# Three reorderings in one kernel: the rounding of an expert chunk on ScalarE, a product on TensorE, an exponential ahead of a rounding

## What is computed

```python
# B=8 batches, S=512 rows, D=512 columns; ctx: 77 rows per batch
x = x + cross_attention(layernorm(x), ctx)       # softmax over one score of the row with its own key (q.k_tok) and 77 with ctx
x = x + ffn(layernorm(x))
def ffn(x):
    q, k, v = (x @ W_qkv + b_qkv) in 16 heads of 32 columns
    attn_out = softmax(q k^T / sqrt(32)) v       # per batch and head, 512 x 512 scores
    gate = softmax(x @ W_gate + b_gate); keep the two largest of 8
    moe_out = sum over the two experts e of gate_e * (x @ W_experts[e] + b_experts[e])
    return attn_out + moe_out
```

## Time and profile before

| | us |
|---|---|
| median of three runs | 1453.66 (1448.44 to 1458.95) |
| the profiled execution | 1453.07 |
| its span, first to last instruction | 1451.4 |
| TensorE busy in the span | 1325.3 |
| VectorE busy | 947.3 |
| ScalarE busy | 910.6 |
| mean granted TensorE clock | 0.962 |

### The profile page before, as it was taken

How to read it: one execution, slowest core, us unless ns; L and a number is a source line. 1 busy time by engine, 2 the same in 40 slices (tenths; PEclk the granted TensorE clock), 3 DMA queues, 4 the chain that set the end, 5 groups by cost and what they waited for, 6 DMA issues and landing times.

```text
span 1451.4 us, 25227 instructions
## 1 busy us (share of the span) xinstructions
PE 1325.3 (91%) x6720; PEld 969.9 (67%) x6721; DVE 947.3 (65%) x2047; ACT 910.6 (63%) x1856; POOL 361.2 (25%) x572
## 2 busy tenths in 40 slices
PE   4989999999799899999999999999998879999987
PEld 4967888888666566656666566665665347777775
DVE  4256788878768878777777777777777623433332
ACT  4123444444338789989899898998999833333332
POOL 0001222222200011210212102120001017777765
PEclk9999999999899999999999999999998779999998
DMA  5005677666664237444464444644449668877873
GB/s 159 1 23 203 244 250 246 244 231 250 211 192 132 51 97 160 95 118 103 105 159 92 119 101 107 159 90 121 101 107 268 233 204 147 144 130 127 144 134 53
DMA packets 111369, 212.44 MB, mean 146 GB/s; under 512 B 28266, under 2 KB 36586, under 8 KB 109140
## 3 DMA queue, kind: packets, MB, share of 16 engines
q1 hardware_dynamic: 82048, 166.13, 38.4%
q0 software_dynamic: 26624, 42.04, 17.3%
q10 hardware_dynamic: 2643, 3.65, 0.8%
HBM read 79.48 MB, written 77.73 MB: 108 GB/s over the span
## 4 chain that ended last, share of the span: by engine, by line
PE 56%; DVE 14%; issue 9%; ACT 8%; DMA 8%; POOL 3%; POOLq 1%; ACTq 0%; DVEq 0%; SPq 0%
PE banks L221 10%; PE banks L223 10%; PE banks L222 10%; PE banks L1073 8%; PE banks L1057 7%; PE banks L1037 7%; DMA out_dram<-plain,score_bias 4%; ACT plain L772 3%; DVE st L1222 3%; ACT banks L762 2%; DMA plain<-h_rows,score_bias 2%; DVE plain L1528 1%; DVE plain L1270 1%; DVE plain L1259 1%; PE banks L1130 1%
## 5 line engine op out<-in xcount | busy, mean ns | idle before, releaser
L221 PE MATMUL banks<-parts 128*128 128x512 f32 (+6 forms) x1108 | 435.4, 393 | 23.6 <-issue 6.6
L223 PE MATMUL banks<-parts 128*128 128x512 f32 (+6 forms) x1108 | 422.1, 381 | 0.0
L222 PE MATMUL banks<-parts 128*128 128x512 f32 (+6 forms) x1108 | 421.8, 381 | 0.0
L1528 DVE TENSOR_REDUCE plain<-banks 128x1 f32<-128x512 f32 x512 | 329.1, 685 | 75.6 <-PE banks L1037 66.0
L762 ACT ACTIVATE banks<-banks,plain 128x512 f32<-128x512 f32 x512 | 339.2, 664 | 25.2 <-DVE plain L1528 23.1
L772 ACT ACTIVATE plain<-banks 128x1024 f32<-128x1024 f32 x256 | 263.0, 1027 | 45.7 <-PE banks L1057 43.9
L221 PEld LDWEIGHTS banks<-parts 128*128 128x128 f32 (+1 forms) x1108 | 213.5, 193 | 66.8 <-issue 33.2
L223 PEld LDWEIGHTS banks<-parts 128*128 128x128 f32 (+1 forms) x1108 | 212.6, 192 | 39.5
L222 PEld LDWEIGHTS banks<-parts 128*128 128x128 f32 (+1 forms) x1108 | 213.7, 193 | 34.1
L1037 PE MATMUL banks<-parts 96*128 96x512 f32 x512 | 207.5, 443 | 23.0 <-ACT banks L762 22.3
L1057 PE MATMUL banks<-parts 104*128 104x512 f32 x512 | 174.6, 423 | 10.3 <-ACT plain L772 10.1
(11 more groups left out here) (180 smaller groups left out, 1495.0 us busy)
## 6 DMA issues: line engine op xcount, KB each, us to landing
parts<-parts SPq DMA_DIRECT2D x384, 128.0 KB, 2.5
experts_split<-parts SPq DMA_DIRECT2D x32, 512.0 KB, 4.2
h_turned<-parts SPq DMA_DIRECT2D x32, 512.0 KB, 2.9
parts<-h_turned SPq DMA_DIRECT2D x32, 512.0 KB, 7.1
parts<-experts_split SPq DMA_DIRECT2D x8, 2048.0 KB, 8.6
plain<-in_x_dram SPq DMA_DIRECT2D x32, 256.0 KB, 4.1
plain<-in_L_ffn_W_experts_dram SPq DMA_DIRECT2D x32, 256.0 KB, 4.2
out_dram<-plain SPq DMA_DIRECT2D x32, 256.0 KB, 2.3
```

What stands on the lines that cost most here:

```text
L221: pe.matmul(out, stat[0], mov[0], start=first, stop=False)
L222: pe.matmul(out, stat[0], mov[1], start=False, stop=False)
L223: return pe.matmul(out, stat[1], mov[0], start=False, stop=last)
L1528: dve.tensor_reduce(nmx[:, k, t:t + 1], bank[SB[t]][:], AX.X, ALU.max, negate=True).then_inc(q["f_max"], 1)
```

## The change

Three places change their order, and nothing is added or removed.

1. In the tile stage ScalarE does `chunk_hi` of tile t directly behind `p_hi` and ahead of `weigh` of the same step; before it was the last work of the step, behind `h2_norm`.
2. In `score` TensorE does the first 512-column chunk of the quadratic form ahead of the eight key products; it was behind them.
3. In the "dense" heads ScalarE does the third exponential E2 ahead of the rounding D; it was behind it.

```diff
             "dense": {"pe": "S0 S1 T2@2 n@1 S2 Da S3 OT T0@1 Db",
-                      "act": "E3@1 t2@2 E0 E1 t0@1 D E2",
+                      "act": "E3@1 t2@2 E0 E1 t0@1 E2 D",
...
             def steps(b, part):
                 for t in range(T):
-                    for d, work in ((-1, p_hi), (0, weigh), (1, h_hi), (2, h_norm), (-2, h2_hi), (-3, gate_out), (-1, h2_norm), (0, chunk_hi)):
+                    for d, work in ((-1, p_hi), (0, chunk_hi), (0, weigh), (1, h_hi), (2, h_norm), (-2, h2_hi), (-3, gate_out), (-1, h2_norm)):
...
+            def own_key(u, c):
+                return prod3(pe, bank[1][:, c * P:D], at(hT[u % 2], sl, c), at(A, sl, c, slice(c * P, D)), c == 0, c == C - 1)
+
             def score(i, u, bb):
 
                 await_ge(pe, "s_step", 4 * i)
                 pe.wait_ge(q["hT_ready"], i + 1)
+                own_key(u, 0)
                 for c in range(C):
...
                 last.then_inc(q["s_keys"], 1)
-                for c in range(C):
-                    last = prod3(pe, bank[1][:, c * P:D], at(hT[u % 2], sl, c), at(A, sl, c, slice(c * P, D)), c == 0, c == C - 1)
+                for c in range(1, C):
+                    last = own_key(u, c)
                 last.then_inc(q["s_full"], 1)
```

## The result

The changed kernel takes 1506.26 us (1504.87 to 1508.78, four executions) against 1452.66 (1448.44 to 1458.95, four) for the kernel before on the same chip: a ratio of 1.037, 95% interval 1.033 to 1.041. The forecast was 1506. The profiled execution took 1504.87 us, its span 1503.2, its mean granted clock 0.944.

What follows compares the result with a forecast made beforehand. It took TensorE to set the tile stage's pace, some 8.6 us a tile, with TensorE and ScalarE nearly level in the heads. Profiled 1453.07 + 56 - 3 = 1506 us; 8-in-10 range 1486 to 1536.

Steps and rivals of the forecast that it cites:

- Part 1, the wait on the load: Tile stage, ScalarE: the moved rounding waits for the chunk's load and delays `weigh`; together +56 us, bounds +41 to +73.
- The loop: Tile stage, per tile: norm to load issue, landing, rounding, `weigh` to next norm; 10.65 us against 8.6, 26 times, +49.6 us.
- The first tiles and the end: Tile stage: tiles 2 to 4, with slower landings, +8 us; from tile 30's exponential to the last value product, -1.6 us.
- both ends of the heads: Head stage rival: bounds of -26 and +16 us come true, whole 1483 or 1525 us; 5% each end, later 5% in all.
- Part 2: Key products in `score`: any gain or loss hidden by ScalarE's loop, 0; at most +3 us were TensorE the bound.
- Part 3: Dense heads: S2's wait replaced by one before `Da`, 0.25 saved in four other heads; -0.4 us a batch, -3 over eight.
- TensorE's busy share: Sign in the profile after: TensorE busy about 77% between 150 and 350 us.
- The clock rival: Tile stage: a 2.4 us wait per tile brings low-clock stretches, 1.1 us a tile, +16 to +32, 1522 to 1538 us; 12%.
- The estimate of the landing: Chunk's 256 KB load: skill gives 2.6 us, a 9.15 us loop, some 16 us cost; set aside for the row's 4.1.

Runs made afterwards that it cites:

- the run with part 3 alone: The kernel before with only the third exponential E2 moved ahead of the rounding D in all dense heads: 1447.55 us, ratio 0.997.

## Why the prediction was right, step by step

- **Part 1, the wait on the load.** Right: the releaser, the place and the size. The loop was put at 10.65 us and is 10.72 (the forecast's terms as printed, 2.8, 4.1, 0.6 and 3.2, add up to 10.7; by them the 26 loops were +51 and the total 1507): 2.68 to the issue (I had 2.8), 4.31 from there to the rounding (4.1 and 0.1), 0.53 and 3.18 (0.5 and 3.2), all medians. 26 loops cost +53.5 us, I had +49.6.
- **What the step left out.** I named one transfer as the one on which the rounding hangs. There are two, and the store lands 0.8 us before the load. The forecast survived since the later one sets the time. The cure that follows from my account is to move the load: directly behind the norm's write it gives nothing (1509), and ahead of it, where the account has no loop left, the kernel stays at 1479, held by the store.
- **The first tiles and the end.** Exponential 4 came 9.3 us later (forecast +8), the last stretch to the fetch for the head stage was 1.3 us shorter (forecast -1.6): 450.21 - 388.69 = +61.5 against +56.
- **The total.** The spans differ by 51.8 us, and the forecast of +53 met them more closely than its terms did. Of the 61.5, 1.7 are given back before the first head, 5.3 in seven batches, and 2.6 between the start of the last batch and the end (374.2 us before, 371.6 after). Of these 2.6 part 3 explains 0.6; that last stretch lies between 373.8 and 376.2 us in the four runs with one or two of the three parts, so the rest I leave as scatter. So the stage came out 5.5 us dearer than forecast, and 1.7 ahead of the heads, 2.9 in them beyond the forecast 3, and that scatter of 2.0 made up for it. That the median agrees with the forecast to 0.3 us is luck; its terms were off by up to 5.5 us. (The chances hold together only with 5% for both ends of the heads; the list of rivals has 5% for each.)
- **Part 2.** Nothing, as forecast, and by itself nothing either.
- **Part 3.** -0.56 us a batch for a forecast of -0.4, so -4.5 for -3; the run with part 3 alone has 0.33%, 4.8 us. Both halves were too small and in the same proportion: I had 4 gains of 0.25 and they are 0.44, 0.26, 0.44 and 0.26, in all 1.40; I had 4 losses of 0.1 to 0.2 and they are 0.16 or 0.27, in all 0.84. The rows behind the earlier trace rows of the changed kernel, ScalarE, VectorE, TensorE:

```profile
696.68 0.66 ACT L762 ACTIVATE banks<-banks,plain 128x512 f32<-128x512 f32 x1
...
697.34 0.69 ACT L719 ACTIVATE parts<-banks,bias_qk_cols 128x512 fp32r<-128x512 f32 x1
```

```profile
698.06 0.75 DVE L1317 SCALAR_TENSOR_TENSOR parts<-banks,bias_qk_cols,parts 128x512 fp32r<-128x512 f32 x1 [0.66 <-ACT parts L719]
```

```profile
697.80 0.23 PE L1050 MATMUL banks<-ident,neg_max_parts 128*104 128x128 f32 x1
697.87 0.44 PE L1041 MATMUL banks<-parts 96*128 96x512 f32 x1
698.87 0.50 PE L221 MATMUL banks<-parts 128*128 128x512 f32 x1 [0.56 <-DVE parts L1317]
699.21 0.39 PE L222 MATMUL banks<-parts 128*128 128x512 f32 x1
```

S2 follows the transposed maxima by 0.07 instead of 0.68 us, the low part follows the start of E2 by 1.38, and `Da` stands still for it. From the maxima to `Da` it is 1.07 us, before 1.02: the wait was exchanged, as forecast. What the sum missed is that the first matmul behind the wait has a pitch of 0.34 us where it was 0.24, and where the interval is 0.27 longer the transposed scores come another 0.11 later at its end.

- **TensorE's busy share.** The forecast of 77% was wrong: 87%. I had counted the matmuls at the full clock. The number to forecast would have been the count of matmuls, which fell by 19%, as 8.59 to 10.72 asks.
- **The clock rival.** Its premise came true, its price did not. The lower level was granted in ten stretches between 150 and 434 us; in the tile stage before it was granted once. Such a stretch, and what stands on either side:

```profile
315.00:324.40 9.40, 6.90 (x39) 5.43 (x38) 5.96 (x20) 2.63 (x6) 2.04 (x8) 1.00 0.63 223
324.40:331.30 6.90, 6.90 (x30) 6.40 (x29) 4.57 (x13) 1.14 (x3) 1.11 (x4) 0.51 0.75 266
331.30:340.00 8.70, 8.70 (x56) 7.46 (x56) 7.00 (x20) 3.68 (x9) 2.04 (x8) 1.00 0.49 178
```

In the 9.4 us ahead of it TensorE stood still for 2.5; then the clock fell from 2.4 to 1.2 GHz (0.51 of full) and it had no wait at all. The tile whose exponential ends this stretch took 10.38 us, the shortest of all 26. Over all 26 tiles the picture is the same: the twelve that share over 2 us with such a stretch have a median of 10.71 us, the other fourteen 10.74, and in each of the 26 the rounding is released by the landing of the load. The stretches take up the wait and nothing else, since TensorE isn't in the loop. The Trainium skill (TensorE: Matmul & The Clock Gate, HAM oscillation) describes a loop of matmuls and waits for a DMA that falls to the low level in every turn; here it fell in about two of five tiles, and the two clocks, 0.90 in the changed kernel and 0.86 in the one with the load moved, went with the same time, 1506 and 1509.
- **The estimate of the landing.** The forecast had set the measured landing of 4.1 us against the estimate of 2.6 from the Trainium skill (DMA: Bandwidth & Descriptors, Anatomy of one DMA) and gone by the row; the changed kernel's landing is 4.2, and the estimate's total of +16 us did not come. The section gives its figures for transfers that GpSimd issues, which the forecast didn't say; these are issued by SyncE.

## What to carry to other kernels

Before you move a step ahead in an in-order engine to fill its idle time, list every semaphore it waits for, and follow each one back to the instruction from which its transfer is issued; an idle engine says nothing of whether the data is there. A double-buffered step has two such waits, the load into its source and the store out of its target, and each that is issued behind a result of the same engine closes a loop whose length is issue + landing + work. Where it turns out late, move the step less far, or the transfers ahead of the wait in their queue: both gave back all of the 54 us lost and left the kernel 19 to 25 us below the one before.

## What the hardware showed beside this

- How long a transfer takes to land depends on what was queued just ahead of it, and moving one moves the others. Median landings between 150 and 350 us, of the changed kernel and then of the one with the store ahead and the load behind the norm's write (KB each, us from issue to landing):

```profile
h_turned<-parts SPq DMA_DIRECT2D x19, 512.0 KB, 2.9
experts_split<-parts SPq DMA_DIRECT2D x19, 512.0 KB, 4.2
h_rows<-plain SPq DMA_DIRECT2D x19, 256.0 KB, 2.0
plain<-in_L_ffn_W_experts_dram SPq DMA_DIRECT2D x19, 256.0 KB, 4.2
```

```profile
experts_split<-parts SPq DMA_DIRECT2D x25, 512.0 KB, 3.1
h_turned<-parts SPq DMA_DIRECT2D x24, 512.0 KB, 3.7
...
h_rows<-plain SPq DMA_DIRECT2D x24, 256.0 KB, 2.0
plain<-in_L_ffn_W_experts_dram SPq DMA_DIRECT2D x24, 256.0 KB, 3.0
```

The same load of 256 KB lands in 4.2 us behind three writes and in 3.0 behind one, and the store of 512 KB in 4.2 behind two others and in 3.1 with only the write of x1 ahead. The transposed rows, now behind the load, go from 2.9 to 3.7.
- A matmul that follows a wait costs TensorE some 0.1 us more than its neighbours. In the head stage of the changed kernel 27 first matmuls of a product (line 221, 512 columns) stand behind a wait of over 0.15 us, and the median from the start of such a one to the next start is 0.34 us (698.87 to 699.21 above), against 0.23 for the 314 without one.
